# An AdaLN, gated recurrence and FFN kernel: the order of the first loads, squares, narrow matmuls and a table load in its opening

## Chip, cores, metric

One core of a Trainium2 chip. The metric is the device time of one launch in microseconds; the median of the runs is what a version is judged by.

## What is computed

Two sequences of 2048 tokens by 512 channels, fp32 in and out. The start of the reference, which is the part that the change touches, is a modulated linear layer whose style comes from a condition vector of each sequence:

```
styles = w @ (affine_w * gain).T + affine_b          # (2, 512), w is cond (2, 256)
ws     = weight[None] * styles[:, None, :]
dcoefs = rsqrt(sum(ws * ws, axis=2) + 1e-8)          # demodulation, (2, 512)
y      = einsum('blc,oc->blo', x * styles[:, None], weight) * dcoefs[:, None]
y      = clip(y + bias, -256, 256)
```

After it come an RMS norm, four 512 by 512 products that feed a gated linear recurrence over the tokens, a second norm with a 512 to 1536 to 512 MLP, and then a second stage of layer norms with embedding gains, an MLP, and an int8-like quantised product. None of that is changed.

## The kernel before

**Tiling.** The 4096 tokens are worked in eight blocks of 512 (`NB`, `BT`), channels on the 128 partitions in four slices (`KT`). Every fp32 product is made of three passes of fp32r: the weight and the data are each split into a high part (ScalarE, a copy) and a low part (VectorE, the difference), and high*high, high*low and low*high are summed in PSUM (`PASSES`). A 128 by 512 product of one weight tile is called wide below.

**Who sets the order.** Each engine runs its own instruction list, in order; semaphores join them. SyncE's queue (SP) and ScalarE's queue (ACT) can both issue transfers. The order of the opening is written out by hand, in one function `prepare` for each engine, which runs before the loop `two_ahead` over the blocks. Nothing in it is planned by a program.

**The opening, engine by engine** (lines of the profile):

- SyncE (`prepare`, L280) issues `vec` (all bias-like columns), `condT` (2 KB) and `aff` = affT (512 KB), waits until cond_wT has landed (`w_loaded[0]`), issues block 0 of x (`load(0)`, 1 MB, L259) and then fc_wT, fc_r_wT (1 MB each, L278), block 1 of x (waits for `x_low` 4), fc_i_wT, fc_gate_wT and ident.
- ScalarE (L587) issues cond_wT (1 MB) first of all, does an Exp and an Ln for the decay rate (L590, L592), splits cond_w high (`split_high(0)`, L570), makes the high part of styled x (`x_early(0)`, L576, which waits for x and for the styles `s_sty`), splits fc_w and fc_r_w high, loads the table for Sqrt by a dummy Sqrt of one column (L597), and evacuates y (`y_early`, L580) once the demodulation factor is there (`s_dem`).
- VectorE (L784) fills constants, then squares slices 2 and 3 of cond_w (L809), makes `sty` from PSUM (L813) and its square `sty2` (L816), and makes the low parts: `split_low(0)` (L780), `x_low_early(0)` (L656), and so on. GpSimd squares slices 0 and 1 (L639) and makes the -0.5 power of the demodulation sums (L641).
- TensorE (L422): `keep_clock(16)`, sixteen matmuls of constants (L402); then the style product, 8 narrow matmuls `aff` x `condT` (L427, two columns wide; the profile shows each as two weight loads and two matmuls) with one constant matmul between the four groups; 3 more constants; then `demodulation(m, k)` (L405), the narrow products of the squared weight with `sty2`, for m = 0 and 1 (eight of them, a constant matmul after every second); then `project_first_high` (L410), 16 wide high*high matmuls (L416) with the eight demodulation products of m = 2 and 3 among them; then the 32 wide matmuls of `project_first_low` (L306, L307) and the 48 of `project_second` for block 1 (L317).

```
keep_clock(16); wait s_cond, s_aff; style product (8, a constant after groups 1 to 3)
keep_clock(3);  wait s_wsq, s_dch, s_sty2; demodulation m=0,1 (8, 4 constants)
project_first_high: 16 wide + demodulation m=2,3 (8);  project_first_low: 32 wide
```

## Time and profile before

| what | value |
|---|---|
| median of 3 runs | 1724.02 us (1723.39 to 1724.2) |
| the profiled execution | 1723.94 us, of which the span of its instructions is 1722.0 us |
| TensorE busy | 1710.7 us, 99% of the span |
| VectorE, ScalarE, GpSimd busy | 73%, 51%, 42% |

The span runs from the first to the last instruction of the program; some 1.9 us of the time lie around it. Times in the trace count from the start of the span.

### The profile page before, as it was taken

What the parts mean: (1) busy time and instruction counts of PE and PEld (TensorE: products, weight loads), DVE (VectorE), ACT (ScalarE), POOL (GpSimd) and SP (SyncE); (2) the same over time, 40 slices, a digit from 0 to 9 for tenths busy, and PEclk for the clock granted to TensorE, in tenths of its full rate; (3) what the DMA queues carried; (4) which work ended last, traced back from release to release, by engine and by line L of the source; (5) the groups of instructions that cost most, each with busy time, mean ns of one, the idle gap of its engine ahead of it and who ended that gap; (6) DMA issues with size and microseconds to landing.
All of it is one profiled execution on the core that took longest, in us unless ns stands there. A gap on an engine that the chain in (4) does not pass through costs nothing. (4 is left out here: it accounts for less than half of the span.)

```text
span 1722.0 us, 23035 instructions
## 1 busy us (share of the span) xinstructions
PE 1710.7 (99%) x7748; PEld 1385.7 (80%) x7756; DVE 1248.9 (73%) x1842; ACT 881.5 (51%) x1306; POOL 728.8 (42%) x642
## 2 busy tenths in 40 slices
PE   9999999999999999999999999999999999999998
PEld 7888888888888888888888888778787787787776
DVE  7766776658989688687464434457997988888876
ACT  7656556556666576575553222233554444543533
POOL 1122221222677465656571000005656755855823
PEclk9999999999999999999999999999999999999999
DMA  6011101120233434232445666887635444535411
GB/s 211 1 49 50 49 0 48 49 74 25 98 123 106 163 99 147 88 119 88 171 147 195 203 212 211 318 298 259 224 113 157 114 140 146 154 103 163 135 43 61
DMA packets 119959, 221.94 MB, mean 129 GB/s; under 512 B 25442, under 2 KB 25890, under 8 KB 119860
## 3 DMA queue, kind: packets, MB, share of 16 engines
q1 hardware_dynamic: 94308, 161.99, 27.8%
q10 hardware_dynamic: 18384, 33.56, 6.1%
q0 software_dynamic: 7168, 25.17, 4.9%
q8 instruction: 49, 0.80, 0.2%
q14 instruction: 50, 0.41, 0.1%
HBM read 158.26 MB, written 58.75 MB: 126 GB/s over the span
## 5 line engine op out<-in xcount | busy, mean ns | idle before, releaser
L1088 PE MATMUL bank<-h_parts,mlp_w 128*128 128x512 f32 x2016 | 459.3, 389 | 0.6 <-ACT product_copy L1308 0.5
L1088 PEld LDWEIGHTS bank<-h_parts,mlp_w 128*128 128x128 f32 x2016 | 378.1, 188 | 80.4 <-ACT product_copy L1308 1.4
L352 PE MATMUL bank<-h_parts,gate_w 128*128 128x512 f32 x1536 | 351.1, 389 | 0.6 <-DVE h_parts L702 0.5
L352 PEld LDWEIGHTS bank<-h_parts,gate_w 128*128 128x128 f32 x1536 | 288.1, 188 | 61.9 <-issue 0.9
L2167 PE MATMUL bank<-operand_parts,int_w 128*128 128x512 f32 x1152 | 274.9, 394 | 0.1
L1153 PE MATMUL bank<-p_parts,mlp_out_w 128*128 128x512 f32 x1152 | 267.4, 391 | 0.0
L2167 PEld LDWEIGHTS bank<-operand_parts,int_w 128*128 128x128 f32 x1152 | 213.7, 188 | 49.4 <-issue 4.8
L1153 PEld LDWEIGHTS bank<-p_parts,mlp_out_w 128*128 128x128 f32 x1152 | 214.7, 188 | 48.0 <-issue 3.4
L1429 POOL TENSOR_TENSOR product_out<-product_out,gelu 128x512 f32<-128x512 f32 x69 | 119.7, 1756 | 95.7 <-DVE product_out L1588 95.1
L627 POOL TENSOR_TENSOR decay_sq<-decay 128x512 f32<-128x512 f32 x32 | 39.2, 1226 | 278.8 <-DVE decay L715 278.8
L1308 ACT ACTIVATE product_copy<-bank,vec_sb 128x512 f32<-128x512 f32 x144 | 99.1, 688 | 107.0 <-PE bank L1088 105.8
L1526 DVE TENSOR_TENSOR p_parts<-p_tile,p_parts 128x512 fp32r<-128x512 f32 x96 | 69.2, 730 | 99.3 <-ACT p_parts L1265 99.3
L1265 ACT ACTIVATE p_parts<-p_tile 128x512 fp32r<-128x512 f32 x96 | 59.8, 630 | 132.3 <-PE bank L1153 114.9
L2642 POOL TENSOR_TENSOR rstds_and_shifts<-rstds_and_shifts,minus_half 128x4 f32<-128x4 f32 x23 | 26.3, 1144 | 198.7 <-DVE rstds_and_shifts L2771 198.3
L2186 PE MATMUL bank<-operand_parts,int_w 128*128 128x512 f32 x384 | 90.1, 393 | 0.0
L2207 PE MATMUL bank<-int_w,hidden_parts 128*128 128x512 f32 x384 | 89.2, 390 | 0.4 <-DVE hidden_parts L2812 0.4
L2207 PEld LDWEIGHTS bank<-int_w,hidden_parts 128*128 128x128 f32 x384 | 71.9, 188 | 16.0 <-ACT hidden_parts L2453 0.8
L2186 PEld LDWEIGHTS bank<-operand_parts,int_w 128*128 128x128 f32 x384 | 72.0, 188 | 15.7
L1516 DVE TENSOR_TENSOR mlp_w<-raw_mlp_w,mlp_w 128x768 fp32r<-128x768 f32 x42 | 44.4, 1057 | 48.1 <-ACT mlp_w L1241 48.1
L634 POOL TENSOR_TENSOR u<-u,y 128x512 f32<-128x512 f32 x32 | 53.8, 1709 | 59.2 <-DVE u L773 59.2
L1417 POOL TENSOR_TENSOR mlp_w_sums<-raw_mlp_w 128x256 f32<-128x256 f32 x42 | 41.5, 989 | 67.1 <-DMA raw_mlp_w<-mlp_gate_g 65.4
L332 PE MATMUL bank<-x_parts,cond_w 128*128 128x512 f32 x288 | 66.3, 389 | 0.0
(322 smaller groups left out, 2733.9 us busy)
## 6 DMA issues: line engine op xcount, KB each, us to landing
p_tile<-p_d ACTq DMA_DIRECT2D x96, 256.0 KB, 4.9
p_d<-product_out SPq DMA_DIRECT2D x92, 256.0 KB, 2.0
raw_mlp_w<-mlp_gate_g SPq DMA_DIRECT2D x21, 512.0 KB, 3.7
raw_mlp_w<-mlp_fc_g SPq DMA_DIRECT2D x21, 512.0 KB, 4.2
xin<-xT SPq DMA_DIRECT2D x8, 1024.0 KB, 6.8
hs_d<-u SPq DMA_DIRECT2D x8, 1024.0 KB, 5.0
hs_pair<-hs_d SPq DMA_DIRECT2D x8, 1024.0 KB, 7.4
x_columns<-xT SPq DMA_DIRECT2D x8, 1024.0 KB, 6.9
```

The lines of the kernel that those rows point to most:

```text
L332: i = pe.matmul(C[m % 2][:], cw[:, s, k, m * P:(m + 1) * P], xr[:, t, k, :], start=k == 0 and n == 0, stop=k == KT - 1 and n == 2)
L352: i = pe.matmul(bank[:], gw[:, w, s, k, m * P:(m + 1) * P], hr[:, q, t, k, :], start=k == 0 and n == 0, stop=k == KT - 1 and n == 2)
L634: pool.tensor_tensor(u[:, m, :], u[:, m, :], y[:, q, m, :], ALU.add).then_inc(hs2_done, 1)
L1088: i = pe.matmul(bank[:], wb[g % 2][:, s, w, kk, :], hop[u % 2][o][:, t, kk, :], start=first and kk == 0 and n == 0, stop=kk == 1 and n == ...
L1153: i = pe.matmul(ACC[b % 2][c][:], ow[j // KT][:, s, j % KT, c * P:(c + 1) * P], pr[n % NPR][:, w, :], start=j == 0 and m == 0, stop=j == F ...
L1265: act.activation(pr[n % NPR][:, 0, :], pt[n % NPT][:], ACT.Copy).then_inc(p_high, 1)
L1308: act.activation(dst[:], src[:], ACT.Identity, bias=v(names[g % 2], 2 * VISITS[g // 2][2] + m)).then_inc(done, 1)
L1429: pool.tensor_tensor(po(i)[t][:], po(i)[t][:], gl[t][:], ALU.mult).then_inc(p_mul, 1)
L1526: dve.tensor_tensor(pr[n % NPR][:, 1, :], pt[n % NPT][:], pr[n % NPR][:, 0, :].bitcast(F32), ALU.subtract).then_inc(p_low, 1)
L2167: i = pe.matmul(A[m][:], w1[OPER[o]][:, a, k, m * P:(m + 1) * P], op[:, s % 4, c, :], start=s == 0 and n == 0, stop=False)
L2186: i = pe.matmul(A[m][:], w1[OPER[o]][:, a, k, m * P:(m + 1) * P], op[:, s % 4, c, :], start=False, stop=s == NS - 1 and n == 2)
L2207: i = pe.matmul(A[t][:], zr[:, a, k, t * P:(t + 1) * P], w2[:, c, k, :], start=k == 0 and n == 0 and not ending, stop=k == KT - 1 and n == 2)
```

## The change

In words. **Transfers:** ScalarE's queue issues five transfers at the start: slices 0 and 1 of cond_wT (`w_half`), affT, slices 2 and 3 of cond_wT (`w_loaded[0]`), slices 0 and 1 of block 0 of x (`x_half`), slices 2 and 3 of it (`x_loaded`). SyncE's queue keeps vec and condT and, instead of loading x, waits also for `x_half` before fc_wT. **Squares:** VectorE takes slices 0 and 2, GpSimd 1 and 3, each starting with the first half. ScalarE's splits and styled x wait by halves. **Constants:** 13 instead of 16 at the start, none between the groups of the style product, two less in the demodulation. **Demodulation:** only m = 0 stands ahead of the high products; m = 1, 2 and 3 (twelve) stand among them, after each of the first three wide matmuls of a slice. **Table:** the dummy Sqrt moves from behind `split_high(2)` to between `split_high(0)` and `x_early(0)`.

```diff
--- before.py
+++ after.py
@@ -225,13 +225,13 @@
         names = ["cond_wT", "fc_wT", "fc_r_wT", "fc_i_wT", "fc_gate_wT"]
         parts = [cw] + [gw[:, n] for n in range(4)]
         w_loaded = [sem(f"w1_loaded{n}") for n in range(5)]
-        w_high, w_low = sem("w1_high"), sem("w1_low")
+        w_half, w_high, w_low = sem("w1_half_loaded"), sem("w1_high"), sem("w1_low")
 
         def w_scale(n, k):
             return v("norm_w", k) if n else 1.0
 
 
-        x_loaded, x_high, x_low = sem("x_loaded"), sem("x_high"), sem("x_low")
+        x_half, x_loaded, x_high, x_low = sem("x_half_loaded"), sem("x_loaded"), sem("x_high"), sem("x_low")
         y_ps, y_evac, y_clip, y_sq = sem("y_ps"), sem("y_evac"), sem("y_clipped"), sem("y_squared")
         cur_done = sem("cur_tab_done")
         sq_high, sq_low = sem("sq_sum_high"), sem("sq_sum_low")
@@ -280,9 +280,8 @@
             def prepare():
                 sp.dma_start(vec[:], ins["vec"]).then_inc(s_vec, 16)
                 sp.dma_start(condT, ins["condT"]).then_inc(s_cond, 16)
-                sp.dma_start(aff, ins["affT"].rearrange("(k p) o -> p k o", p=P)).then_inc(s_aff, 16)
                 sp.wait_ge(w_loaded[0], 16)
-                load(0)
+                sp.wait_ge(x_half, 16)
                 load_weights(1)
                 load_weights(2)
                 load(1)
@@ -408,36 +407,33 @@
                     i.then_inc(s_dem_ps, 1)
 
             def project_first_high():
-                narrow = [(m, k) for m in (2, 3) for k in range(KT)]
+                narrow = [(m, k) for m in range(1, KT) for k in range(KT)]
                 for k in range(KT):
                     pe.wait_ge(w_high, k + 1)
                     pe.wait_ge(x_high, k + 1)
                     for m in range(KT):
                         pe.matmul(YB[0][m][:], cw[:, 0, k, m * P:(m + 1) * P], XP[0][:, 0, k, :], start=k == 0, stop=False)
-                        if (KT * k + m) % 3 < 2 and narrow:
+                        if m < KT - 1:
                             demodulation(*narrow.pop(0))
 
             def prepare():
                 pe.wait_ge(s_dch, 3)
-                keep_clock(16)
+                keep_clock(13)
                 pe.wait_ge(s_cond, 16)
                 pe.wait_ge(s_aff, 16)
                 for m in range(KT):
                     for k in range(2):
                         i = pe.matmul(I[0][:, 2 * m:2 * m + 2], aff[:, k, m * P:(m + 1) * P],
                                       condT[:, 2 * k:2 * k + 2], start=k == 0, stop=k == 1)
-                    if m < KT - 1:
-                        keep_clock(1)
                 i.then_inc(s_sty_ps, 1)
                 keep_clock(3)
                 pe.wait_ge(s_wsq, 2)
                 pe.wait_ge(s_dch, 7)
                 pe.wait_ge(s_sty2, 1)
-                for m in range(2):
-                    for k in range(KT):
-                        demodulation(m, k)
-                        if k % 2:
-                            keep_clock(1)
+                for k in range(KT):
+                    demodulation(0, k)
+                    if k % 2:
+                        keep_clock(1)
                 project_first_high()
                 for m in range(KT):
                     project_first_low(m)
@@ -565,14 +561,20 @@
                         early(5)
 
             def split_high(n, ks=range(KT)):
-                act.wait_ge(w_loaded[n], 16)
+                if n == 0:
+                    act.wait_ge(w_half, 16)
                 for k in ks:
+                    if n or k == 2:
+                        act.wait_ge(w_loaded[n], 16)
                     act.activation(parts[n][:, 0, k], raw[:, n, k], ACT.Copy, scale=w_scale(n, k)).then_inc(w_high, 1)
 
             def x_early(b):
-                act.wait_ge(x_loaded, 16 * (b + 1))
                 act.wait_ge(s_sty, BATCH)
+                if b == 0:
+                    act.wait_ge(x_half, 16)
                 for k in range(KT):
+                    if k == (0 if b else 2):
+                        act.wait_ge(x_loaded, 16 * (b + 1))
                     act.activation(XP[b][:, 0, k, :], xin[:, k, :], ACT.Copy, scale=sty[:, k, 0:1]).then_inc(x_high, 1)
 
             def y_early(b, m):
@@ -585,16 +587,21 @@
                 act.activation(hf[:, m, :], y[:, 0, m, :], ACT.Square).then_inc(y_sq, 1)
 
             def prepare():
-                act.dma_start(raw[:, 0], ins[names[0]].rearrange("(k p) o -> p k o", p=P)).then_inc(w_loaded[0], 16)
+                cond_w = ins[names[0]].rearrange("(k p) o -> p k o", p=P)
+                act.dma_start(raw[:, 0, 0:2], cond_w[:, 0:2]).then_inc(w_half, 16)
+                act.dma_start(aff, ins["affT"].rearrange("(k p) o -> p k o", p=P)).then_inc(s_aff, 16)
+                act.dma_start(raw[:, 0, 2:KT], cond_w[:, 2:KT]).then_inc(w_loaded[0], 16)
+                act.dma_start(xin[:, 0:2], xT[:, 0:2, 0:BT]).then_inc(x_half, 16)
+                act.dma_start(xin[:, 2:KT], xT[:, 2:KT, 0:BT]).then_inc(x_loaded, 16)
                 act.wait_ge(s_abs, 1)
                 act.activation(sp_t[1], sp_t[0], ACT.Exp, scale=-1.0).then_inc(s_sp, 1)
                 act.wait_ge(s_sp, 1)
                 act.activation(sp_t[2], sp_t[1], ACT.Ln, bias=1.0).then_inc(s_sp, 1)
                 split_high(0)
+                act.activation(small[:, 62:63], quarter, ACT.Sqrt)
                 x_early(0)
                 split_high(1)
                 split_high(2)
-                act.activation(small[:, 62:63], quarter, ACT.Sqrt)
                 act.wait_ge(s_dem, 1)
                 act.wait_ge(s_dem_ps, 1)
                 y_early(0, 0)
@@ -634,8 +641,8 @@
                     pool.tensor_tensor(u[:, m, :], u[:, m, :], y[:, q, m, :], ALU.add).then_inc(hs2_done, 1)
 
             def prepare():
-                pool.wait_ge(w_loaded[0], 16)
-                for k in range(2):
+                for k in (1, 3):
+                    pool.wait_ge((w_half, w_loaded[0])[k // 2], 16)
                     pool.tensor_tensor(wsq[:, k], raw[:, 0, k], raw[:, 0, k], ALU.mult).then_inc(s_wsq, 1)
                 pool.wait_ge(s_dem_in, 1)
                 pool.tensor_tensor(small[:, 20:28], small[:, 20:28], mhalf, ALU.pow).then_inc(s_dem, 1)
@@ -775,8 +782,8 @@
             def split_low(n, ks=range(KT)):
                 for k in ks:
                     dve.wait_ge(w_high, KT * n + k + 1)
-                    if n == 0 and k < 2:
-                        dve.wait_ge(s_wsq, k + 1)
+                    if n == 0 and k % 2:
+                        dve.wait_ge(s_wsq, (k + 1) // 2)
                     dve.scalar_tensor_tensor(out=parts[n][:, 1, k], in0=raw[:, n, k], scalar=w_scale(n, k),
                                              in1=parts[n][:, 0, k].bitcast(F32), op0=ALU.mult,
                                              op1=ALU.subtract).then_inc(w_low, 1)
@@ -804,8 +811,8 @@
                 dve.tensor_tensor(sp_t[0], v("alpha"), sp_t[3], ALU.max).then_inc(s_abs, 1)
                 dve.tensor_scalar(half_b[:, 0:KT], v("fc_r_b"), 0.5, None, ALU.mult)
                 dve.tensor_scalar(half_b[:, KT:2 * KT], v("fc_i_b"), 0.5, None, ALU.mult).then_inc(s_c4, 1)
-                dve.wait_ge(w_loaded[0], 16)
-                for k in range(2, KT):
+                for k in (0, 2):
+                    dve.wait_ge((w_half, w_loaded[0])[k // 2], 16)
                     link(dve.tensor_tensor(wsq[:, k], raw[:, 0, k], raw[:, 0, k], ALU.mult))
                 dve.wait_ge(s_sty_ps, 1)
                 pv = I[0][:, 0:8].rearrange("p (k b) -> p k b", b=BATCH)
```

## Rows read from the trace of the kernel before

**Rows 1.** One stretch of the run: length, busy us (instructions) by engine, PEclk, DMA share, GB/s.

```profile
60.00:1722.00 1662.00, 1654.14 (x7495) 1340.18 (x7501) 1201.76 (x1748) 839.30 (x1242) 720.01 (x632) 1.00 0.39 128
```

**Rows 2.** Timeline, opening, issues of DMAs: start us, us, engine, line, op, tiles.

```profile
0.74 0.49 ACTq L588 DMA_DIRECT2D attn_stage<-cond_wT  x1
...
1.19 0.42 SPq L282 DMA_DIRECT2D small<-condT  x1
...
1.66 0.43 SPq L283 DMA_DIRECT2D y<-affT  x1
...
6.38 0.38 SPq L259 DMA_DIRECT2D xin<-xT  x1
...
6.80 0.51 SPq L278 DMA_DIRECT2D attn_stage<-fc_wT  x1
```

**Rows 3.** DMAs issued in 0 to 45 us: tiles, queue, KB, us from issue to landing.

```profile
attn_stage<-cond_wT ACTq DMA_DIRECT2D x1, 1024.0 KB, 5.6
...
small<-condT SPq DMA_DIRECT2D x1, 2.0 KB, 5.4
...
y<-affT SPq DMA_DIRECT2D x1, 512.0 KB, 6.0
...
xin<-xT SPq DMA_DIRECT2D x3, 1024.0 KB, 5.3
...
attn_stage<-fc_wT SPq DMA_DIRECT2D x1, 1024.0 KB, 7.6
```

**Rows 4.** Timeline, PE, five looks at the constant matmuls: start us, us to the last one's end, count.

```profile
2.28 6.17 PE L402 MATMUL bank<-h_parts,ones_mean 128*128 128x512 f32 x16 [2.28 <-DVE h_parts L798]
...
4.58 1.05 PE L402 MATMUL bank<-h_parts,ones_mean 128*128 128x512 f32 x2
...
5.43 1.05 PE L402 MATMUL bank<-h_parts,ones_mean 128*128 128x512 f32 x2
...
7.13 0.85 PE L402 MATMUL bank<-h_parts,ones_mean 128*128 128x512 f32 x3
...
7.59 0.62 PE L402 MATMUL bank<-h_parts,ones_mean 128*128 128x512 f32 x2
```

**Rows 5.** Timeline, opening, weight loads of PE: start us, us, engine, line, tiles, count.

```profile
8.06 0.64 PEld L427 LDWEIGHTS bank<-small,y 128*128 128x128 f32 x4
...
8.73 0.65 PEld L427 LDWEIGHTS bank<-small,y 128*128 128x128 f32 x4
...
11.47 0.52 PEld L405 LDWEIGHTS bank<-small,h_full 128*128 128x128 f32 x4 [0.29 <-issue]
...
14.06 0.19 PEld L416 LDWEIGHTS bank<-x_parts,cond_w 128*128 128x128 f32 x1
...
19.52 0.19 PEld L306 LDWEIGHTS bank<-x_parts,cond_w 128*128 128x128 f32 x1
```

**Rows 6.** Timeline, opening, the other engines: start us, us, ..., idle before and its releaser.

```profile
6.43 2.99 POOL L639 TENSOR_TENSOR h_full<-attn_stage 128x512 f32<-128x512 f32 x2 [5.99 <-DMA attn_stage<-cond_wT]
...
6.57 2.17 ACT L570 ACTIVATE cond_w<-attn_stage 128x512 fp32r<-128x512 f32 x4
...
10.93 0.23 DVE L813 SCALAR_TENSOR_TENSOR small<-bank,vec_sb 128x4 f32<-128x4 f32 x2 [2.41 <-PE bank L427]
...
11.66 2.56 ACT L576 ACTIVATE x_parts<-xin,small 128x512 fp32r<-128x512 f32 x4 [2.92 <-DMA xin<-xT]
```

**Rows 7.** Timeline, 18 to 21 us, ACT and POOL.

```profile
18.93 2.10 POOL L641 TENSOR_TENSOR small<-small 128x8 f32<-128x8 f32 x1 [9.51 <-DVE small L825]
...
19.59 1.28 ACT L597 ACT_TABLE_LOAD   x1
...
20.89 0.20 ACT L597 ACTIVATE small<-small 128x1 f32<-128x1 f32 x1
```

**Rows 8.** DMAs issued in 924.4 to 927 us: queue, KB each, median us to landing.

```profile
x_columns<-xT SPq DMA_DIRECT2D x1, 1024.0 KB, 12.5
...
p_tile<-p_d ACTq DMA_DIRECT2D x2, 256.0 KB, 6.0
```

## Prediction

> **What bounds the kernel now.** I read the stretches first. From 60 us on TensorE is busy for 1654.14 of 1662 us [rows 1]: what the opening gains or loses is passed on one for one, as a shift of everything behind it. So the change is worth what it does to the moment at which TensorE starts its dense work. A measurement of this kernel can tell about 0.2% (3.4 us) from no change; the stretch that is edited is 20 us long.
>
> Then the timeline along TensorE. It runs constants up to 8.06, the style product from 8.06, demodulation from 11.47, the high products from 14.06 and the low products from 19.52 [rows 5]. It hardly stands, but part of that is filling: what sets 19.52 is the order of its own instructions, and two things it waits for, the style (sty, which VectorE begins at 10.93 [rows 6]) and styled x (ScalarE begins at 11.66, released by the transfer of x; 2.56 for four slices, the first some 0.7 [rows 6], so there at 12.4). TensorE comes to the high products only at 14.06. So its own list is the bound, not x, with 1.7 us between them.
>
> **The change part by part.** Sums are against the profiled execution, 1723.94 us, of which the span is 1722.0; the median of the runs is 0.08 us above it.
>
> Three constants less at the start. They start 0.43 us apart (two from 4.58 to 5.43) and then 0.23 (two from 7.13 to 7.59): 1.2 and 2.4 GHz, though the clock column reads 1.00 throughout. The sixteen end at 2.28 + 6.17 = 8.45, the last lasting 0.39, so it starts at 8.06; four starts at 0.23 lie between 7.13 and it, and the thirteenth is at 7.36 [rows 4]. The three that go are of the fast kind: 3 x 0.23 = **0.70 us**, if affT and condT are there by 7.4. Bounds: nothing (they are late) and 0.70.
>
> Transfers. Before, cond_wT landed at 0.74 + 5.6 = 6.3, condT, issued at 1.19, only at 1.19 + 5.4 = 6.6, affT at 1.66 + 6.0 = 7.7 and x at 6.38 + 5.3 = 11.7 [rows 2, 3]. In a busy queue half a megabyte thus takes 7.7 - 6.3 = 1.3 to 1.4 us. In the new order: first half of cond_w at 5.0, affT 6.4, all of cond_w 7.7 (the same 1.5 MB that had landed by 7.7 before), first half of x 9.0, second 10.4. x comes 1.3 us sooner, since it is not issued only once cond_w has landed. SyncE's new wait for x_half moves fc_wT from 6.80 to about 9.1. It then finds the engines free, takes the 5.3 us of an x from an idle queue [rows 3] instead of 7.6, and lands at 14.4 as before (6.8 + 7.6). Queued behind it are fc_r_wT, which follows as before, and block 1's x, which waits for the low parts in any case. Cost nothing; if fc_w came a microsecond late, ScalarE's eight splits of it and of fc_r_w, which ended at 19.59 [rows 7], would end past 20.0, when the first y is due. That is their cover.
>
> condT is the odd one: 2 KB that took 5.4 us and came through 0.2 us behind cond_w, a transfer of the other queue issued 0.45 us before it. I take it that it gets in behind the one large transfer ahead of it, now half as long, so at 5.0 to 6.4. At 926 us ScalarE's small loads landed 6.0 us after their issue while SyncE's last large load, issued then, took 12.5 [rows 8]: a small transfer is not held until the other queue is empty. The Trainium skill ("DMA: Bandwidth & Descriptors", section "Issuing engines are not separate DMA queues") has transfers interleave whichever engine issues them; by that condT would have landed well before cond_w, and the trace does not agree. The sum is the same by page or row; what the row adds is rival (c).
>
> Style product without constants between its groups. A group of four loads and its constant takes 8.73 - 8.06 = 0.67. Four narrow loads with no constant ahead span 0.52, the last lasting 0.19, so they are 0.11 apart [rows 5]: 0.44 for a group, 0.23 for the constant. Three less: **0.68 us** (at least 3 x 0.07, if the gap to the next group stays). sty then starts at 10.93 - 0.70 - 0.68 = 9.55.
>
> Squares. GpSimd's two took 2.99 from 6.43 [rows 6], 1.5 each. Now they run from 5.0 and from 7.7, to 9.2; VectorE's no longer. VectorE needs to be free at 9.55, TensorE needs all four at 10.1. Cost nothing.
>
> ScalarE. The splits of cond_w took 2.17 for four [rows 6]; the last two now wait for 7.7 and end at 8.9. Then the moved table load: from load to dummy 20.89 - 19.59 = 1.30 [rows 7], and 0.1 to the next: 10.3. Styled x starts then rather than at 11.66 (sty is there at 9.8, x at 9.0), so its first slice is ready at 11.05 and one more every 0.6. A rule speaks against this place: the Trainium skill ("ScalarE: Activation LUTs", section "What ACT_TABLE_LOAD costs") puts a drain of some 1.4 us on top of the 1.28 for each switch of tables. By it the slice would come 1.4 later, at 12.4, and the sum would be about 0.7. The row has the load and the next instruction 1.30 apart, so I keep that.
>
> Demodulation. Half of it, two groups of four loads and a constant, goes from ahead of the high products: 2 x 0.67 = **1.35 us** less. TensorE comes to them at 14.06 - 0.70 - 0.68 - 1.35 = 11.3; the slice is there at 11.05. Four products come back among the high ones. These took 19.52 - 14.06 = 5.46 for 16 wide and 8 narrow products [rows 5]; 16 x 0.23 = 3.7, so 0.22 for a narrow one (two loads at 0.11), and four cost **0.90 us**. Bounds: 0, if they hide, and 0.90; the rows say they don't.
>
> Demodulation now ends just ahead of the last wide matmul, at about 17.8; GpSimd's power takes 2.10 behind it [rows 7], so till 20.1 or 20.2. The first y is due when TensorE has made eight low matmuls, 17.7 + 8 x 0.23 and some 0.4 of drain, 20.0. A wait of 0.1 to 0.2 on ScalarE, then, with the other y behind it; but TensorE writes that bank again only after all 32 low matmuls, at 25. Cost nothing; what is late next would be the second y, due at 21.8, with 0.8 us between.
>
> **Sum:** 0.70 + 0.68 + 1.35 - 0.90 = 1.83 us. The low products start at 17.7 and all behind them shifts by as much: 1723.94 - 1.83 = 1722.1; with the 0.08 of the median 1722.2, 0.1% less.
>
> **The rivals.**
>
> (a) ScalarE or a transfer becomes the bound. Between the styled slice (11.05) and TensorE (11.3) lie 0.25 us. If all of cond_w lands later than 8.0, or the table switch takes longer, every us more is lost whole: with cond_w at 8.5 to 9.0 the gain is 1.3 to 0.8; with the page's drain 0.7. So 1722.7 to 1723.3. For: five transfers may cost some tenths more than two. Against: the same bytes had landed by 7.7.
>
> (b) Narrow products hide among wide ones: 2.7 less, 1721.3. Against: 0.22 each in this very stretch, and the slice at 11.05.
>
> (c) The other side: condT is held until ScalarE's queue is empty. It lands 0.2 behind the second half of x, 10.6. Style starts then instead of at 8.06; sty at 10.6 + 2.87 - 0.68 = 12.8; high products at 12.8 + 3.13 - 1.35 = 14.6, low ones at 14.6 + 5.46 + 0.9 = 20.9: 1.4 us later than before, 1725.4. TensorE would also stand from 7.6 to 10.6, and if its clock goes back to 1.2 GHz for as long as at the start (2.28 to 7.13, 4.85 us), half of that is lost: 2.4, so 1727.8. It costs from the point at which condT lands behind 7.4, and turns the sign behind 7.4 + 1.83 = 9.2. For: in the opening it came out behind all that the other queue had issued. Against: rows 8.
>
> (d) The clock alone: thirteen constants end little behind its rise at 7.13, and no wide one stands in the style product. If it rises later, or falls in the narrow stretch, up to 2.4 us are lost: 1724.6 at most, 1722.7 for a rise half a microsecond later. Against: before, it held through the same narrow groups. The Trainium skill ("TensorE: Matmul & The Clock Gate", section "What's actually happening") has activity release the clock; what narrow matmuls count for, no row here shows.
>
> (e) The opening is shorter but the dense work is not earlier, because something behind 19.52 (the norm of block 0, a weight) sets it: 1724.0. Against: each of these is fed by the low products and shifts with them.
>
> **How the numbers follow.** Forecast (gain 1.5 to 2.0) 0.47; (a) 0.22; (b) 0.04; (c) 0.11, half of it with the clock; (d) 0.10; (e) 0.06. The time is the forecast's, 1722.2 us; its own range is 1721.8 to 1722.8, with 0.2 for the scatter of a median. It takes (b), (a), and the milder part of (d) and (e) with their scatter to hold 8 in 10: 1721.3 to 1724.3. Faster by over 0.2% would need 3.4 us, more than is removed: 0.03. Slower by over 0.2% is (c) with the clock: 0.06. Within: 0.91.
>
> **What would show it.** In the changed profile: condT landing by 7.4; the first style load at 7.4, sty at 9.55; the table load on ScalarE at 8.9, styled x from 10.3; the first high matmul's load at 11.3, the first low one's at 17.7, 1.83 sooner than 19.52; the first gated product sooner by as much; a span near 1720.2. It is wrong if TensorE stands ahead of the style product (condT or affT) or of the first high matmul (table load or x), if matmuls start 0.43 us apart behind 8 us (the clock), or if the low products come sooner and the gated products do not.

## The result, and the profile after

The changed kernel takes 1729.05 us (median of 22 runs, 1721.88 to 1731.95) against 1724.02 us (median of 22, 1723.39 to 1724.99). The comparison recorded with these runs gives a ratio of 1.0021, 95% interval 1.0013 to 1.0029. The median is the better guide here, because the runs are of separate kinds with nothing in between: 7 lie from 1721.88 to 1723.09, 7 from 1728.72 to 1729.39 and 8 from 1730.31 to 1731.95. A third of the runs does what the change was meant to do (their median is 1722.89, 1.1 us under the kernel before) and two thirds cost 5 to 8 us against it. The profiled run is of the middle kind: 1729.2 us, a span of 1727.1.

Stretches of the changed kernel's profile: length, busy us (instructions) of PE, PEld, DVE, ACT, POOL, then the granted clock, DMA share and GB/s.

```profile
6.00:9.00 3.00, 3.00 (x23) 2.73 (x21) 0.85 (x2) 2.63 (x6) 1.77 (x2) 1.00 1.06 395
9.00:12.00 3.00, 2.48 (x15) 1.93 (x15) 2.90 (x9) 2.97 (x6) 0.23 (x1) 1.00 0.62 158
12.00:15.00 3.00, 3.00 (x15) 2.59 (x15) 3.00 (x6) 1.27 (x3) 0.00 (x0) 0.68 1.01 370
15.00:18.00 3.00, 3.00 (x12) 2.62 (x11) 1.98 (x3) 2.83 (x5) 0.00 (x0) 0.50 1.00 328
...
21.00:24.00 3.00, 3.00 (x11) 2.52 (x10) 1.74 (x4) 0.00 (x0) 1.50 (x1) 0.50 1.05 395
24.00:27.00 3.00, 3.00 (x9) 2.38 (x8) 2.40 (x4) 0.61 (x1) 0.60 (x1) 0.54 0.63 230
27.00:30.00 3.00, 3.00 (x15) 2.45 (x14) 0.57 (x2) 1.73 (x4) 1.04 (x1) 1.00 0.02 6
```

The column to read is the clock. It is full up to 12 us, falls inside 12:15, stays at one half (1.2 GHz) for the next nine microseconds and is full again behind 27. The busy column says nothing of this: TensorE is busy for 3.00 of 3.00 us in every row but 9:12. Beside it the same stretch of both kernels, first before, then changed: all of it busy, 74 matmuls against 44.

```profile
13.00:26.70 13.70, 13.70 (x74) 11.77 (x73) 11.17 (x20) 11.72 (x18) 3.14 (x2) 1.00 0.90 321
...
13.00:26.70 13.70, 13.70 (x44) 11.58 (x43) 8.12 (x13) 5.70 (x10) 2.10 (x1) 0.50 0.95 345
```

Another stretch answers to [rows 1]: behind 60 us it is busy 1658.97 of 1667 us, 8.0 us of pauses as before, so nothing else was lost there.

Up to the fall the chain is nearly the one that was forecast. Timeline of the changed kernel, in order of time; the rows of before are [rows 5] and [rows 6].

```profile
2.28 5.10 PE L401 MATMUL bank<-h_parts,ones_mean 128*128 128x512 f32 x13 [2.28 <-DVE h_parts L805]
...
6.98 1.99 PEld L426 LDWEIGHTS bank<-small,y 128*128 128x128 f32 x16
...
8.22 1.56 DVE L816 TENSOR_TENSOR h_full<-attn_stage 128x512 f32<-128x512 f32 x1 [2.15 <-DMA attn_stage<-cond_wT]
8.89 0.54 PEld L401 LDWEIGHTS bank<-h_parts,ones_mean 128*128 128x128 f32 x3
...
9.32 1.28 ACT L601 ACT_TABLE_LOAD   x1
...
9.81 0.23 DVE L820 SCALAR_TENSOR_TENSOR small<-bank,vec_sb 128x4 f32<-128x4 f32 x2
...
10.36 0.52 PEld L404 LDWEIGHTS bank<-small,h_full 128*128 128x128 f32 x4 [0.93 <-issue]
...
10.72 2.55 ACT L578 ACTIVATE x_parts<-xin,small 128x512 fp32r<-128x512 f32 x4
...
11.59 0.19 PEld L415 LDWEIGHTS bank<-x_parts,cond_w 128*128 128x128 f32 x1
...
13.70 0.76 PEld L404 LDWEIGHTS bank<-small,h_full 128*128 128x128 f32 x2
```

The style product starts 1.08 us sooner and takes 1.9 us without one wide matmul in it. Of the 1.08, 0.70 is the three constants that are gone; the rest comes from the clock, which first rises at 6.2 us in this profile and at 7.1 in that of before (constants start 0.43 us apart until then, 0.23 behind). The style (9.81) comes 0.03 us behind VectorE's second square (8.22 + 1.56), and TensorE's weight loads pause 0.93 us before demodulation (its matmuls, which end later than their loads, only 0.53: every pause below has these two readings). The high products start at 11.59 instead of 14.06. From 13.70 on the pair of narrow weight loads of one demodulation product spans 0.76 us instead of 0.42: that is the half clock. The low products, forecast for 17.7, start at 22.2.

The transfers in the changed kernel's profile (the rows of before are [rows 3]):

```profile
attn_stage<-cond_wT ACTq DMA_DIRECT2D x2, 512.0 KB, 5.5
xin<-xT ACTq DMA_DIRECT2D x2, 512.0 KB, 7.6
...
y<-affT ACTq DMA_DIRECT2D x1, 512.0 KB, 5.5
...
small<-condT SPq DMA_DIRECT2D x1, 2.0 KB, 4.4
```

condT, issued at 1.19, lands at 5.6, right behind the first half of cond_w and not behind the five. affT lands at 6.8, x by halves at 9.5 and 10.8 where it was 11.7. So the transfers did what was asked.

### The profile page after: what moved, and what is told of

Read it like the earlier page. It is cut to its first block and busy times, and to the rows that moved or that the text cites. A ratio compares the mean times of both kernels' runs of the same rounds, so it can differ in the third digit from the quotient of the medians.

```text
span 1727.1 us, 23023 instructions
## 1 busy us (share of the span) xinstructions
PE 1715.0 (99%) x7740; PEld 1389.1 (80%) x7748; DVE 1248.9 (72%) x1842; ACT 881.5 (51%) x1306; POOL 733.9 (42%) x642
```

## The experiments

Each ran 5 to 12 times. "Falls" counts runs that lie more than 2 us above the fast kind, or, where no run is fast, above the kernel before less 1 us. The expectations name theories. In short, theory 1 is that wide matmuls became too few over the whole stretch, theory 2 that the style product without constants does it, theory 3 that the narrow products among the high ones do. The kernel before was run beside each group: 1723.55 us beside e1 to e4, 1724.02 beside e5 to e8, 1724.35 beside e9 to e11 and 1724.47 beside e12. Its own level thus moves by 0.9 us from chip to chip, and a gain is read against the one beside it. Its 121 runs lie from 1723.1 to 1725.3, but for one at 1726.38 beside e12; the kinds of the changed kernel it does not show. (The recorded expectations count 16 falls in 22 runs of the changed kernel; it is 15.)

**e1, constants back** (changed kernel):

```diff
-                keep_clock(13)
+                keep_clock(16)
...
+                    if m < KT - 1:
+                        keep_clock(1)
```

> The changed kernel with only its constants at the start and in the style product put back (16 at the start, one between the groups of the style product); demodulation stays spread among the high products. Theory 1 (the clock falls because too few wide matmuls run between 7 and 14 us, and what tips it is the whole thinning, of which the pause of 0.5 us at 9.9 and the spread demodulation are the later part): some runs still fall to 1.2 GHz, so times of two kinds, near 1724 and near 1730. Theory 2 (the 1.7 us of style product without a constant is what tips it): no run falls, all runs within 0.5 us of 1723.6 (the changed kernel's fast kind, 1722.5, plus 1.4 us of constants, less what hides in the pause). Theory 3 (the twelve narrow products among the high ones tip it): falls as often as the changed kernel, 16 of 22.

Measured: 1723.79 us (1723.11 to 1724.58), no fall in 11 runs. Six constants cure it, the spread demodulation staying as it is: theory 3 falls. Theory 1 had some runs falling here, so as it was put it missed too; theory 2 had none. But with the six constants the change is worth nothing (+0.2 against its kernel before, inside the interval 0.9993 to 1.0011).

**e2, demodulation back** (changed kernel; m = 0 and 1 ahead with four constants, eight narrow products among the high ones):

```diff
-                for k in range(KT):
-                    demodulation(0, k)
-                    if k % 2:
-                        keep_clock(1)
+                for m in range(2):
+                    for k in range(KT):
+                        demodulation(m, k)
+                        if k % 2:
+                            keep_clock(1)
...
-                narrow = [(m, k) for m in range(1, KT) for k in range(KT)]
+                narrow = [(m, k) for m in (2, 3) for k in range(KT)]
...
-                        if m < KT - 1:
+                        if (KT * k + m) % 3 < 2 and narrow:
```

> The changed kernel with only the demodulation put back as before (m = 0 and 1 ahead of the high products with four constants, eight narrow products among them); thirteen constants at the start and none in the style product stay. Theory 1: fewer runs fall than in the changed kernel, perhaps none, as two constants more stand behind the pause. Theory 2: falls as often as the changed kernel, near 1729 to 1731. Theory 3: no run falls, all near 1723.0 (1722.5 plus 1.35 less 0.90).

Measured: 1728.22 us, 10 falls in 10 runs, five near 1727 and five near 1730. Putting demodulation back does not help; if anything it is worse than 15 of 22. Theory 1 had expected fewer falls, for two constants more behind the pause, and missed; theory 2 had this right. In this profile the matmuls stand 1.08 us ahead of demodulation, twice the changed kernel's pause.

**e3, constants gone from the kernel before** (the reverse edit of e1, on the kernel before, and nothing else):

> The kernel before with only its constants taken away (13 at the start, none between the groups of the style product); transfers, squares, table load and demodulation as before. Styled x is released by its transfer at 11.7 and demodulation fills the time before it, so without a fall the time should be 1.4 us less, 1722.6. Theory 1: two kinds of runs or none that falls. Theory 2: many runs fall, near 1728 to 1730. Theory 3: none falls.

Measured: 1730.43 us, 5 falls in 5 runs. The whole loss is there without the five transfers, the table load, the squares or the spread demodulation: **taking the constants away is sufficient**. Theory 2 expected it, theory 1 only some runs or none. Its profile also shows where. The weight loads around the style product, which here waits for affT (0.59 us by the matmuls):

```profile
7.95 1.93 PEld L427 LDWEIGHTS bank<-small,y 128*128 128x128 f32 x16 [1.00 <-issue]
9.76 0.97 PEld L402 LDWEIGHTS bank<-h_parts,ones_mean 128*128 128x128 f32 x3
```

The three constants' loads behind the style product already span 0.97 us instead of the 0.54 of the changed kernel: the clock fell at 9.7, at the end of a pause and sixteen narrow loads, before demodulation had begun. In the changed kernel it fell at 13.1, when the first four demodulation products were done and the high products had begun. So there is more than one place at which a run can be caught, which may be why the fallen runs come in more than one size.

**e4, the pause filled** (changed kernel, between the style product and demodulation):

```diff
-                keep_clock(3)
+                keep_clock(6)
```

> The changed kernel with three constants more (six instead of three) between the style product and demodulation, where TensorE paused for 0.5 us; they take 0.7 us and end about when the pause did. Theory 1: no run or few runs fall, and the time is that of the changed kernel's fast kind, 1722.3 to 1723.0, which would beat both kernels. Theory 2: falls about as often as before the filling, as the style product has still no constant in it. Theory 3: the same, falls as often.

Measured: 1722.63 us (1721.77 to 1723.32), no fall in 11 runs; 0.9 us under its kernel before (1723.55), ratio 0.9994 (0.9985 to 1.0003). Three constants in time that TensorE did not use are enough, although the style product has none in it: theory 2 in its strict form falls too, and here theory 1 had it right. No theory as written forecasts e1 to e4 together; what all four agree on is that the constants decide. The same stretches as above, of this kernel:

```profile
9.00:12.00 3.00, 2.94 (x17) 2.34 (x17) 2.90 (x10) 2.97 (x6) 0.00 (x0) 1.00 0.56 199
12.00:15.00 3.00, 3.00 (x20) 2.71 (x20) 3.00 (x5) 1.61 (x4) 0.00 (x0) 1.00 0.98 356
15.00:18.00 3.00, 3.00 (x21) 2.67 (x20) 1.54 (x3) 2.97 (x5) 0.00 (x0) 1.00 0.95 330
```

21 matmuls in 15:18 where the changed kernel made 12 with the same busy time. The low products start at 18.05 and the first gated product at 38.94; in the changed kernel's profile 22.23 and 45.24. The fall costs 6.3 us there, and all of it arrives in the time.

**e5, the table load behind the styled x** (e4 with the dummy Sqrt one line later, behind `x_early(0)`):

> The kernel with the pause filled (six constants ahead of demodulation), and the dummy Sqrt with its table load moved from ahead of the styled x to just behind it, where ScalarE waits for fc_w anyway (it stood 1.8 us there in the changed kernel). If the table load on ScalarE's path is what holds the high products (styled x began at 10.7 to 11.0, its first half had landed at 9.0 to 9.5 and the style was there at 9.6 to 10.0), styled x begins near 10.0 and the first high matmul comes 0.4 to 0.8 us sooner: 1722.0 against 1722.6 for the filled kernel. If TensorE's own list or the squares hold it, no difference. In either case the clock should hold; if it falls in some runs, the filled kernel is close to the edge.

Measured: 1722.88 us, no fall in 11; against its kernel before (1724.02) 1.1 us less, as e4 within what can be told, and not the 0.6 us better than e4 that was expected if the table load held the high products. From the first load of demodulation to the first high one its profile has 1.35 us (10.67 to 12.02), e4's 1.77 (10.04 to 11.81): there TensorE's loads waited 0.34 us for styled x behind the table load. In the changed kernel's profile it is 1.23 (10.36 to 11.59), no wait at all. The table load is a near tie, worth some tenths at most.

**e6, demodulation back in the filled kernel** (e4 with the edit of e2):

> The filled kernel with the demodulation as in the kernel before (m = 0 and 1 ahead with four constants, eight narrow products among the high ones). By the sum of the prediction the move is worth 1.35 - 0.90 = 0.45 us, less what TensorE then waits for styled x: 1722.6 to 1723.1 here. If narrow products among the wide ones cost more or less than 0.22 each, the low products show it: they should start 0.45 us later than in the filled kernel, or no later at all if x holds the high products there. The clock holds, as more constants run.

Measured: 1723.51 us, no fall in 11, 0.5 us under its kernel before where e4 was 0.9 under its own, and 0.45 was forecast for the move. But that agreement is luck: the median span, from first to last instruction, is 1720.8 us here and in e5, whose runs stand beside the same kernel before (1721.8), so between these two the move shows no gain in the span, and the times differ by what lies around it. What the move is worth in the whole is not shown. Its profile has the two prices: demodulation's loads from 10.52 to the first high one at 13.13 are 2.61 us, and the high products, to 18.59, are 5.46 [rows 5: 2.59 and 5.46]. e4's took 18.05 - 11.81 = 6.24 with four narrow products more, 0.20 each; e5's 18.38 - 12.02 = 6.36, 0.22 each.

**e7, transfers back in the filled kernel** (cond_wT whole on ScalarE's queue; affT and x on SyncE's, x behind cond_wT; splits and squares released by whole transfers):

> The filled kernel with the transfers as before (cond_wT whole in ScalarE's queue; vec, condT, affT, then x after cond_wT in SyncE's), squares and splits released by the whole transfers. affT lands near 7.7, so TensorE stands some 0.7 us ahead of the style product; styled x begins at 11.7 to 11.9, the high products near 12.5 instead of 11.8: 0.7 us more than the filled kernel, 1723.3, if the clock holds. Theory 1 (a stretch with a pause and narrow matmuls and too few wide ones lets the clock fall) says that this pause sits right in the narrow stretch and that many runs fall, near 1730. A theory in which only the pause ahead of demodulation counts says none falls.

Measured: seven runs from 1724.45 to 1725.16 and 4 falls in 11 (1731.23 to 1732.97). The seven are not a clean kind. Four of them have a mean granted clock of 0.998, and none of the runs of the kernel before beside these experiments is under 0.999. Only one has a clock of 1.000, with a span of 1721.6 us, where the other six have 1722.6 to 1722.8. So most of these runs seem to hold a short fall that the count leaves out; none of them was profiled. The middle of the seven is 0.6 over its kernel before and e4 0.9 under, 1.5 us apart, but that is not the price of the transfers. By the clean run's span it is 0.8 (0.2 under its kernel before's 1721.8, where e4's median span is 1.0 under), close to the 0.7 expected and from one run.

Six constants no longer suffice with the old transfers, as theory 1 had said. That TensorE's standing ahead of the style product does it is argued and not shown. A row from its profile, a fallen run, in which the loads stand 0.61 us there and the matmuls 0.10:

```profile
8.08 1.86 PEld L427 LDWEIGHTS bank<-small,y 128*128 128x128 f32 x16 [0.61 <-issue]
9.86 1.23 PEld L402 LDWEIGHTS bank<-h_parts,ones_mean 128*128 128x128 f32 x6
```

**e8, only the demodulation spread** (kernel before with the demodulation of the change):

> The kernel before with only the demodulation moved (m = 0 ahead, twelve narrow products among the high ones); all constants, transfers and the table load as before. Styled x is released by its transfer at 11.7, its first slice at 12.4, while TensorE would be ready at 12.7: 0.45 us less than before, 1723.3, if the clock holds. Theories 1 and 2: it holds, since every constant stands. Theory 3 (narrow products among the wide ones tip it): runs near 1730.

Measured: 1723.99 us, no fall in 11, equal to its kernel before (1724.02). So theory 3 falls again. Expected was 1723.3. Its profile has the low products at 18.81 instead of 19.52, and that run took 1723.18, the lowest of the eleven; why the median shows none of it (the median spans are equal too, 1721.8) stays open.

**e9, only the style constants back** (changed kernel with the second hunk of e1):

> The changed kernel with only the three constants between the groups of the style product put back (13 at the start). They take 0.7 us and delay the style product's end to about 9.7, near where the second square ends anyway, so they should cost 0 to 0.7. Theory 1 (what counts is how many wide matmuls run in the whole stretch from the style product to the high products, so any three constants put there cure it): no run falls, 1722.6 to 1723.3. Theory 1b (only the pause and the demodulation behind it count, so constants must stand behind 9 us): some runs still fall, near 1730.

Measured: 1723.13 us, no fall in 11; 1.2 us under its kernel before (1724.35), ratio 0.9993 (0.9985 to 1.0002). Another place for three constants, the same cure and, within what can be told, the same gain as e4; theory 1 had it right. They cost next to nothing, since the style waits for VectorE's square anyway: in its profile the style product's last load ends at 9.4, the square at 9.6, and the style comes at 9.64.

**e10, only the start's constants back** (changed kernel with the first hunk of e1):

> The changed kernel with only the start's constants put back (16 instead of 13), none between the groups of the style product. They run ahead of the narrow stretch and push the style product back by 0.7 us, so the pause behind it shrinks or goes. Theory 1: fewer runs fall than in the changed kernel (16 of 22), but not none, since the 1.8 us of style product without a constant and the demodulation stay; fallen runs near 1729 to 1731, the others near 1723. Theory 4 (the clock falls only because the pause of 0.5 us is there): none falls.

Measured: ten runs from 1722.52 to 1723.64, and 2 falls in 12 (1731.49, 1731.83). Three constants at the start thus help (15 of 22 fell without them) but do not cure. Whether they do less than three inside the sparse part is likely and not settled: 2 of 12 against none of 11 is little. In its profile, of a run that held, demodulation's matmuls follow the constants without a pause (these end at 10.80, those start at 10.68; in the changed kernel 9.87 and 10.39). So the pause alone (theory 4) is unlikely to be it, unless a transfer was late in just those two runs; e11 speaks against it more plainly.

**e11, all narrow products first** (changed kernel; sixteen demodulation products ahead without constants, high products dense):

```diff
-                for k in range(KT):
-                    demodulation(0, k)
-                    if k % 2:
-                        keep_clock(1)
+                for m in range(KT):
+                    for k in range(KT):
+                        demodulation(m, k)
...
-                        if m < KT - 1:
-                            demodulation(*narrow.pop(0))
```

> The changed kernel with all sixteen demodulation products ahead of the high products, no constants among them, and the high products back to back. It makes the narrow stretch longer (16 products, 3.6 us) and the stretch behind it dense. Nearly all runs should fall. If narrow products among the wide ones are what keeps the clock down for so long once it has fallen (13.65 us in the changed kernel's profile, while TensorE was busy all the time), it rises sooner here, after 7 to 10 us, and a fallen run costs 3 to 5 us instead of 6 to 8: 1726 to 1728. If the fall's length does not depend on what runs, the fallen runs are near 1729 to 1731 again.

Measured: 1728.31 us, 11 falls in 11, but smaller ones (1726.20 to 1727.20 and 1728.31 to 1729.16). Stretches of its profile; the columns are those above.

```profile
6.00:9.00 3.00, 3.00 (x20) 2.63 (x18) 1.05 (x1) 2.81 (x6) 1.76 (x2) 1.00 1.06 394
9.00:12.00 3.00, 3.00 (x19) 2.67 (x18) 2.88 (x10) 2.97 (x6) 0.00 (x0) 0.75 0.64 201
...
15.00:18.00 3.00, 3.00 (x12) 2.75 (x12) 2.78 (x6) 2.91 (x5) 0.89 (x1) 0.50 1.01 308
18.00:21.00 3.00, 3.00 (x9) 2.34 (x8) 3.00 (x5) 1.99 (x4) 1.21 (x1) 0.54 1.04 397
21.00:24.00 3.00, 3.00 (x15) 2.47 (x14) 0.01 (x1) 0.00 (x0) 0.00 (x0) 1.00 1.04 380
```

Two readings. First, the clock falls inside 9:12 (at 10.5) although TensorE's matmuls stand nowhere in the six microseconds of the first two rows: a pause is not needed for a fall. This, more than e10, speaks against theory 4.

Second, the wide matmuls are dense from 16.55 and the clock is back just before 21, 4.2 us later. In the changed kernel they are dense only from 22.0, with the last high product, and it is back at 26.7, 4.7 us later. The other fallen profiles (e2, e3, e7, e12) have it back 2.5 to 3.7 us behind the start of their dense part, so there is no fixed delay; but in none of the six does it come back among high products that have narrow ones between them, though TensorE was busy in every microsecond of these. That nothing else shifts the return was not tried.

**e12, the style ahead of the square** (e9 with three edits: VectorE squares slice 2 behind the style, TensorE takes slice 2 last, one constant instead of three ahead of demodulation, table load as in e5):

```diff
-                keep_clock(3)
+                keep_clock(1)
...
-                for k in range(KT):
-                    demodulation(0, k)
-                    if k % 2:
+                for k in (0, 1, 3, 2):
+                    if k == 2:
+                        pe.wait_ge(s_dch, 7)
+                    demodulation(0, k, 2)
+                    if k in (1, 2):
```

> The kernel with the style constants put back (e9), and three edits more: VectorE makes the style and its square ahead of its second square of cond_w (slice 2), TensorE takes slice 2 last in the first four demodulation products, one constant instead of three stands between the style product and them, and the table load for Sqrt stands behind the styled x. In the changed kernel VectorE's style waited for that square (it ended 0.03 us ahead of it). If that square is what held the style, and the constants what holds the first demodulation product, the style begins 0.3 us and the high products 0.3 to 0.6 us sooner than in e9, and the time is 0.3 to 0.5 us less: 0.1% under the kernel before. If x or the squares hold the high products instead, it equals e9. The clock should hold in all runs, because the wide high products move up by what the constants leave; if it falls in some, the two constants were needed.

Measured: 1729.32 us, 7 falls in 7. Its style product has all its constants; what it lacks is two constants behind it, where the loads now pause:

```profile
10.36 0.19 PEld L401 LDWEIGHTS bank<-h_parts,ones_mean 128*128 128x128 f32 x1
11.19 0.76 PEld L404 LDWEIGHTS bank<-small,h_full 128*128 128x128 f32 x4 [0.64 <-issue]
```

The expectation that the clock holds missed. The two constants that are gone are the likely cause, as e9 holds with them; but the order of the squares and of the first four demodulation products and the table load changed too, and neither the reordering with the constants left in nor the constants alone taken from e9 was tried.

## Why the prediction was wrong

The forecast was 1722.2 us and a range to 1724.3; the median came out at 1729.05, on the other side.

**The step that failed** is rival (d), "The clock alone", in its chance and in its price, and with it the way in which the main sum treats constants. In the sum, "three constants less at the start" and "style product without constants between its groups" are pure savings of 0.23 us each, and the only condition set was that affT and condT be there in time. I asked what hides a removed cost, but not what a removed filler had been holding up. (d) gave that 0.10 on the ground that "before, it held through the same narrow groups". They were not the same groups: the first three had a wide matmul behind each, and those were what the change took out. e3 shows that this alone, with three fewer at the start, makes all 5 runs fall; e9, e4 and e1 that putting three or six back makes none of 11 fall in each. What decides between a run that falls and one that holds in the changed kernel, 15 to 7, no run shows.

**The price** "up to 2.4 us" was taken from the 4.85 us that TensorE ran at half clock at the start. Measured, the fallen runs cost 4.7 to 7.9 us. The stretch at half clock is not everywhere as long as at the start. There dense constants ended it; behind the fall came high products thinned by narrow ones, and the half clock lasted 13.65 us in the profile and cost 6.3 us against e4. e11 fell with dense high products behind it, had 10.2 us at half clock and cost less (4.0 us over its kernel before, against 5.0). That twelve narrow products instead of eight among the high ones make it longer is not shown: with eight it lasted 13.65 us in e2 and 17.1 in e3.

The Trainium skill ("TensorE: Matmul & The Clock Gate", section "HAM oscillation — how this bites in real kernels") lays such falls to idle gaps in which TensorE waits. That is not what these profiles show. Their matmuls pause between the first rise and the fall by 1.08 us in e2, 0.6 in e3, 0.5 in the changed kernel, 0.4 in e12, 0.1 in e7 and not at all in e11, and the clock falls in each. In the changed kernel's profile TensorE was busy 6.28 of the 6.80 us from 6.2 to 13.0, and its single pause ended 2.7 us before the fall. What e1, e4 and e9 have more than the changed kernel is wide matmuls and nothing else, and none of their runs falls: it is these that held the clock, whatever the busy column says.

**What was right**, and is seen wherever the clock holds:
- The dense work behind the opening passes everything on: 6.3 us lost at the first gated product, 6.2 us in the span, against e4's.
- The narrow product among wide ones at 0.22 (0.20 in e4, 0.22 in e5) and the second half of demodulation at 1.35 (half of it takes 1.35 in e5, the whole 2.61 in e6).
- condT behind the one large transfer ahead of it and not behind the whole queue, so rival (c) did not happen.
- The table load at 1.30 to the next instruction (9.32 to 10.61). The Trainium skill ("ScalarE: Activation LUTs", section "What ACT_TABLE_LOAD costs") has a further drain at each such switch; the trace has none, neither behind the load nor ahead of it, where the last split had ended at 9.29.

**Sizes that were off.** In the fast kind the gain is 1.1 us, not 1.83. The style product started at 6.98 instead of 7.4, and that was luck (the clock rose at 6.2 in this profile) and bought nothing, since the style then waited for the square. Transfers land 0.3 to 0.5 us later than summed (cond_w 8.1, not 7.7; fc_w, issued at 9.56, 15.1 and not 14.4). So VectorE's second square ends at 9.78, and the style comes at 9.81 instead of 9.55; "VectorE's no longer", said of the square at 1.5 us, put it at 9.2; it took 1.56 beside GpSimd's square, so its length was right and its start late. Styled x starts at 10.72 instead of 10.3 and the high products at 11.59 instead of 11.3. With e4's low products at 18.05 that leaves 1.47 us of the 1.83 at that point in its profile, 1.46 at the first gated product (38.94 against 40.40), and 1.0 in its span (1720.99 against 1721.99). Most of the last half microsecond is in TensorE's pauses behind 60 us, 8.25 in e4's profile against 7.86 in that of before, which is within what one profile of each differs by.

**What is better than the change:** e4, e5 and e9, the changed kernel with three constants in time that TensorE does not use. Each holds in 11 of 11 runs, and they stand 0.9, 1.1 and 1.2 us under the kernel before. That they beat that one too is likely and not shown, since each interval still takes in 1.

## What to carry to other kernels

A matmul that computes nothing may still hold the clock: before taking one out, ask not only what it costs but what the engine runs around it, and do not take a busy column at 100% as a sign that the clock will hold. Run such a change many times, since a profile or three runs may catch one kind only. If filler must go, take it from a dense part and leave it in the sparse one (e9), or put it where the engine would stand anyway, where it is nearly free (e4). Narrow products spread among wide ones are cheap at full clock (0.2 us each), but in no profile here did a fallen clock rise among them. And before comparing two profiles line by line, look when the clock first rose in each: here it alone moved the start of the style product by some tenths.

## What the runs showed of the hardware

- One program has several speeds. Whether TensorE's clock fell differed from run to run: 15 of 22 in the changed kernel, 4 of 11 in e7, 2 of 12 in e10. In the profiles the first rise came at 5.4 to 8.0 us of the span, with constants running from 2.3 in every one. Profiles with a fall have it from 5.4 to 8.0 and those without from 5.8 to 7.4, so an early or late rise does not tell which will fall.
- A core at half clock reads 3.00 busy of 3.00 us. The clock column and the spacing of the weight loads (0.42 to 0.76 for a pair) tell. Ahead of the first rise the column does not either: it reads 1.00 while the constants start 0.43 us apart.
- The fallen runs of one kernel come in two groups: near 1729 and 1731 us in the changed kernel, 1727 and 1730 in e2, 1726.5 and 1728.5 in e11. The half clock lasted 10.2 us in e11's profile, 13.65 in those of the changed kernel and e2, 17.1 in e3's, e7's and e12's.
- A 2 KB transfer in one queue landed 0.2 us behind the large one that the other queue had issued just before: at 6.6 behind 1 MB, at 5.6 behind half of it.
